# A mixture-of-experts decoder layer: residual rows kept in an array of sums, experts' outputs added to it by scatters

## What is computed

```python
x = _layernorm(x + attn(x, Wq, Wk, Wv, Wo, bo))
x = _layernorm(x + retention(x, ctx, ctx))
logits = x @ gate                       # 8 experts
weights, selected = top_k(logits, 2);  weights = softmax(weights)
g = x @ experts_w1[e];  u = x @ experts_w3[e]
eo[e] = (silu(g) * u) @ experts_w2[e]
x = _layernorm(x + sum over the two selected e of weight[e] * eo[e])
```

## Time and profile before

| | |
|---|---|
| median of 3 runs | 1004.99 us (1000.88 to 1008.09) |
| the profiled execution: time | 1007.5 us |
| its span in the profile | 1005.7 us |
| granted clock of PE over the span | 0.915 of full speed |
| PE busy | 804.7 us, 80% |
| DVE busy | 790.3 us, 79% |
| POOL busy | 652.6 us, 65% |
| ACT busy | 613.4 us, 61% |
| moved by DMA | 72.55 MB |

### The profile page before, as it was taken

One profiled execution on the slowest core, in us unless ns is written; L12 is line 12 of the kernel. 1 busy time (PEld: TensorE's weight loads), 2 busy tenths in 40 slices (PEclk: granted clock), 3 DMA queues, 4 the chain that ended last, 5 costly groups with the idle time before them and its releaser, 6 DMA issues.

```text
span 1005.7 us, 34508 instructions
## 1 busy us (share of the span) xinstructions
PE 804.7 (80%) x11940; PEld 603.2 (60%) x11940; DVE 790.3 (79%) x2155; ACT 613.4 (61%) x1416; POOL 652.6 (65%) x738
## 2 busy tenths in 40 slices
PE   1667799989999899898868660999999999999500
PEld 1345465656656556656544430799999999999500
DVE  4797799988999988998846644688888888888475
ACT  1133566768767777676666851676667666766355
POOL 0349767799999999998996456245444544454443
PEclk9788799999999999999987965899999999999855
DMA  9312222123232232221212004222222222222176
GB/s 307 81 29 54 40 48 50 42 62 70 51 71 62 54 74 52 61 58 42 63 39 62 23 22 91 58 61 66 63 62 61 66 63 61 62 65 58 53 252 226
DMA packets 145300, 72.55 MB, mean 72 GB/s; under 512 B 75024, under 2 KB 134544, under 8 KB 145136
## 3 DMA queue, kind: packets, MB, share of 16 engines
q1 hardware_dynamic: 124800, 40.43, 17.4%
q0 software_dynamic: 8640, 17.84, 5.4%
q10 hardware_dynamic: 11696, 12.08, 3.8%
HBM read 41.98 MB, written 28.34 MB: 70 GB/s over the span
## 4 chain that ended last, share of the span: by engine, by line
PE 38%; POOL 32%; issue 12%; DVE 3%; DMA 3%; ACT 2%; POOLq 0%; SPq 0%; ACTq 0%; DVEq 0%
POOL prod_ev L1536 17%; POOL routed_rows L1553 11%; PE QKV L773 9%; PE ST L773 9%; PE XT L801 6%; PE SC L801 5%; POOL rs L1516 3%; PE YY L589 2%; DMA prod_ev<-token_halves 2%; PE SC L560 1%; PE YY L791 1%; PE TR L791 1%; PE TR L606 1%; DMA routed_rows<-xe,pos 1%; PE TR L603 1%
## 5 line engine op out<-in xcount | busy, mean ns | idle before, releaser
L1536 POOL TENSOR_TENSOR prod_ev<-e_sb,q_v 128x512 f32<-128x512 f32 x256 | 300.2, 1206 | 70.5 <-PE YY L589 35.6
L1585 POOL DMA_INDIRECT token_halves<-w_new,tok_i x142 | 137.8, 971 | 32.5 <-issue 22.2
L1553 POOL DMA_INDIRECT routed_rows<-xe,pos x128 | 129.6, 1013 | 30.6 <-issue 29.9
L1151 DVE TENSOR_TENSOR prod_qk<-q_v,QKV 128x2048 f32<-128x2048 f32 x64 | 144.7, 2273 | 4.5 <-ACT q_v L870 4.5
L1438 DVE TENSOR_TENSOR prod_ev<-prod_qk,prod_ev 128x1024 f16<-128x1024 f32 x71 | 87.0, 1226 | 56.0 <-ACT prod_ev L1028 56.0
L1028 ACT CAST prod_ev<-prod_qk 128x1024 f16<-128x1024 f32 x71 | 74.2, 1045 | 76.0 <-DVE prod_qk L1464 51.4
L773 PE MATMUL QKV<-k_t,w_hl 128*128 128x256 f16 x852 | 116.8, 274 | 0.1
L773 PE MATMUL ST<-k_t,w_hl 128*128 128x256 f16 x852 | 116.7, 273 | 0.0
L409 POOL TENSOR_TENSOR marks<-half_c 128x1 f32<-128x1 f32 x103 | 19.9, 193 | 142.2 <-DVE w_new L1454 142.0
L1464 DVE SCALAR_TENSOR_TENSOR prod_qk<-ST,hid_scale,prod_qk 128x512 f32<-128x512 f32 x142 | 99.6, 744 | 2.3 <-ACT prod_qk L1037 2.3
L1037 ACT ACTIVATE prod_qk<-QKV,silu_scale 128x512 f32<-128x512 f32 x142 | 96.1, 678 | 8.6 <-PE QKV L773 4.6
(11 more groups left out here) (169 smaller groups left out, 1695.3 us busy)
## 6 DMA issues: line engine op xcount, KB each, us to landing
w_new<-routed_rows SPq DMA_DIRECT2D x71, 130.0 KB
prod_ev<-token_halves SPq DMA_DIRECT2D x16, 512.0 KB, 5.1
x_sb<-x SPq DMA_DIRECT2D x32, 128.0 KB, 3.0
x_res<-x SPq DMA_DIRECT2D x128, 32.0 KB
head_rows<-o_n SPq DMA_DIRECT2D x32, 128.0 KB
o_t<-head_rows SPq DMA_DIRECT2D x64, 64.0 KB
ctx_sb<-ctx SPq DMA_DIRECT2D x32, 128.0 KB, 2.7
out<-prod_qk ACTq DMA_DIRECT2D x16, 256.0 KB, 4.0
```

Of the source, the lines that this page charges most:

```text
L1151: eng.tensor_tensor(prod_qk[:, u, :, :].rearrange("p d (i j) -> p d i j", j=NH), q.unsqueeze(3).to_broadcast([P, HD, NH, NH]), k.unsqueeze ...
L1536: ins = eng.tensor_tensor(prod_ev[:, u, q, :, :, 0:HD], e_sb[:, it.slot(2), u, 64 * q:64 * q + 64].rearrange("p (i j) -> p j i", j=4).unsq ...
L1553: eng.indirect_dma_start(out=xs, out_offset=bass.IndirectOffsetOnAxis(ap=pos[:, r, 2 * u + k:2 * u + k + 1], axis=0), in_=xe[:, r, u, k, : ...
L1585: eng.indirect_dma_start(out=halves, out_offset=bass.IndirectOffsetOnAxis(ap=tok_i[:, s, u:u + 1], axis=0), in_=yw[:, s, u, :], in_offset= ...
```

## The change

The two half rows of a token in DRAM are gone. In their place stands `token_sums` with one row for each token. In stage A, SP writes the second norm's rows there once, four transfers a duo, 15 steps behind its first load. In stage B the experts' outputs, without `xh`, are added to these rows by POOL's scatters: the DMA reads the row, adds and writes it back. Since the two experts of a token can be in neighbouring tiles, each tile's scatters wait until those of the tile before have landed. In stage C one row a token is loaded (256 KB a chunk, ring of 8), DVE's addition is gone, and all 16 chunks are written out.

```diff
-        "spare_ids": 2 * n_tok + p[:, None] + P * np.arange(4 * n_exp)[None, :],
-        "ids": 2 * (P * b + row)[:, None] + 4 * P * (ids // 4) + 2 * S * (ids // 2 % 2) + ids % 2,
+        "spare_ids": n_tok + p[:, None] + P * np.arange(4 * n_exp)[None, :],
+        "ids": (P * b + row)[:, None] + 2 * P * (ids // 4) + S * (ids // 2 % 2),
...
-    PE_LAGS, ACT_LAGS, DVE_LAGS, POOL_LAGS, SP_LAGS = 13, 13, 14, 11, 9
-    CTX_LAG, HEADS_LAG = 9, 8
+    PE_LAGS, ACT_LAGS, DVE_LAGS, POOL_LAGS, SP_LAGS = 13, 13, 14, 11, 15
+    CTX_LAG, HEADS_LAG, ROWS_LAG = 9, 8, 15
...
-    C_FIRST, C_LAGS = 8, 3
+    C_RING = 8
+    C_FIRST, C_LAGS = n_chunks_c, 3
...
-    halves = nc.dram_tensor("token_halves", [2 * n_tok + 2 * n_exp * TILE, P], F32).ap()
+    token_sums = nc.dram_tensor("token_sums", [n_tok + 2 * n_exp * TILE, P], F32).ap()
...
+                if it := at(ROWS_LAG):
+
+                    r = it.slot(RING)
+                    wait(it, x2_ready)
+                    wait_dma(it, x2_out, 1, 64)
+                    for u in range(2):
+                        for b in range(2):
+                            eng.dma_start(x2_rows[it.number()][u][b], xe[S * u:S * u + S, r, b, 0, 0:P]).then_inc(x2_out, 16)
...
+            eng.wait_ge(x2_out, 64 * n_duo)
...
-                    wait(c, fout_ready, RING)
-                    eng.dma_start(fin[:, c.slot(RING), :, :, :],
-                                  half_rows[:, bass.ds(c.number() * C_SLICES, C_SLICES), :, :]).then_inc(fin_in[c.slot(RING)], 16)
+                    wait(c, fout_ready, C_RING)
+                    eng.dma_start(fin[:, c.slot(C_RING), :, :],
+                                  sum_rows[:, bass.ds(c.number() * C_SLICES, C_SLICES), :]).then_inc(fin_in[c.slot(C_RING)], 16)
...
                 wait_ring(it, routed_out, RING, 64)
+                wait_dma(it, x2_out, RING, 64)
...
-                    wait_ring(t, xg_in)
-                    wait(t, yw_ready, RING)
-                    eng.mul(xh[:, t.slot(RING), :, :], xg[:, t.slot(RING), :, 0:P], 0.5).then_inc(xh_ready, 1)
...
-                        ins = eng.scalar_tensor_tensor(out=yw[:, s, u, :], in0=YB[t.slot(2)][:, P * u:P * u + P],
-                                                       scalar=wt[:, s, u:u + 1], in1=xh[:, s, u, :], op0=ALU.mult, op1=ALU.add)
+                        ins = eng.tensor_scalar(yw[:, s, u, :], YB[t.slot(2)][:, P * u:P * u + P], wt[:, s, u:u + 1], None, ALU.mult)
...
-                    eng.tensor_tensor(y[:, :, 0, :], y[:, :, 0, :], y[:, :, 1, :], ALU.add).then_inc(fsum_ready, 1)
-                    wait(c, fsum_ready)
...
+                    wait_ring(t, half_out, 1, 32)
                     for u in range(2):
-                        eng.indirect_dma_start(out=halves, out_offset=bass.IndirectOffsetOnAxis(ap=tok_i[:, s, u:u + 1], axis=0),
-                                               in_=yw[:, s, u, :], in_offset=None).then_inc(half_out[s], 16)
+                        eng.indirect_dma_start(out=token_sums, out_offset=bass.IndirectOffsetOnAxis(ap=tok_i[:, s, u:u + 1], axis=0),
+                                               in_=yw[:, s, u, :], in_offset=None, compute_op=ALU.add).then_inc(half_out[s], 16)
```

More of the change, by code:

```diff
@@ L216, in build @@
     x_rows = x.rearrange("(n u b h g) d -> n u b g h d", u=2, b=2, h=NH, g=4)
-    half_rows = halves[0:2 * n_tok, :].rearrange("(p n k) d -> p n k d", p=P, k=2)
+    sum_rows = token_sums[0:n_tok, :].rearrange("(p n) d -> p n d", p=P)
+    x2_rows = token_sums[0:n_tok, :].rearrange("(n u b h g) d -> n u b g h d", u=2, b=2, h=NH, g=4)
     out_rows = out.rearrange("(p n) d -> p n d", p=P)
@@ L312, in in_new @@
             return w_new[:, at * RING * 2:(at + c) * RING * 2].rearrange("p (r u c) -> p r u c", r=RING, u=2)
-        xg, yw, xh = in_new(0, ROW), in_new(ROW, P), in_new(ROW + P, P)
+        xg, yw = in_new(0, ROW), in_new(ROW, P)
         x_hl = k_t[:, 0:2, :, :].rearrange("p r u t -> p (r u t)").bitcast(F16).rearrange("p (s k t) -> p s k t", s=2, k=2)
@@ L323, in build @@
         tok_i = sb("tok_i", [RING, 2], I32)
-        fin = stage_b2[:, 0:RING * C_SLICES * 2 * P].rearrange("p (r n k d) -> p r n k d", r=RING, n=C_SLICES, k=2)
+        fin = stage_b2[:, 0:C_RING * C_SLICES * P].rearrange("p (r n d) -> p r n d", r=C_RING, n=C_SLICES)
         fout = stage_b[:, 0:RING * C_SLICES * P].rearrange("p (r n d) -> p r n d", r=RING, n=C_SLICES)
@@ L380, in build @@
         x_in, ctx_in, routed_out = (ring_sem(n) for n in ("x_in", "ctx_in", "routed_out"))
+        x2_out = sem("x2_out")
         y_in = ring_sem("y_in")
@@ L389, in build @@
             [sem(f"{n}{half}") for half in range(2)] for n in ("g_done", "u_done", "sil_ready", "hid_ready"))
-        xhi_ready, xlo_ready, xh_ready, hhi_ready, hlo_ready = (
-            sem(n) for n in ("xhi_ready", "xlo_ready", "xh_ready", "hhi_ready", "hlo_ready"))
+        xhi_ready, xlo_ready, hhi_ready, hlo_ready = (
+            sem(n) for n in ("xhi_ready", "xlo_ready", "hhi_ready", "hlo_ready"))
         yw_ready, tok_ready, wt_ready = (sem(n) for n in ("yw_ready", "tok_ready", "wt_ready"))
-        fin_in, fin_out = ring_sem("fin_in"), ring_sem("fin_out")
+        fin_in, fin_out = [sem(f"fin_in{i}") for i in range(C_RING)], ring_sem("fin_out")
         fnb_ready = sem("fnb_ready")
-        fsum_ready, fstat_ready, fmv_ready, fve_ready, frs_ready, fout_ready = (
-            sem(n) for n in ("fsum_ready", "fstat_ready", "fmv_ready", "fve_ready", "frs_ready", "fout_ready"))
+        fstat_ready, fmv_ready, fve_ready, frs_ready, fout_ready = (
+            sem(n) for n in ("fstat_ready", "fmv_ready", "fve_ready", "frs_ready", "fout_ready"))
         marks = sb("marks", [7])
@@ L503, in load_tile @@
                     wait(t, xgt_done, RING)
-                    wait(t, xh_ready, RING)
                     wait(t, wt_ready, RING)
@@ L1047, in last_norm @@
                     for n in range(C_SLICES):
-                        ins = eng.activation(fout[:, r, n, :], fin[:, r, n, 0, :], ACT.Identity,
+                        ins = eng.activation(fout[:, r, n, :], fin[:, c.slot(C_RING), n, :], ACT.Identity,
                                              bias=fnb[:, s, n:n + 1], scale=frs[:, s, n:n + 1])
@@ L1449, in tile_step @@
                     wait(t, down_done)
-                    wait(t, xh_ready)
                     wait(t, wt_ready)
@@ L1471, in last_norm @@
                     s = c.slot(2)
-                    y = fin[:, c.slot(RING), :, :, :]
-                    wait_ring(c, fin_in)
-                    eng.tensor_tensor(y[:, :, 0, :], y[:, :, 0, :], y[:, :, 1, :], ALU.add).then_inc(fsum_ready, 1)
-                    wait(c, fsum_ready)
+                    eng.wait_ge(fin_in[c.slot(C_RING)], 16 * (c.off // C_RING + 1))
                     wait(c, fmv_ready, 2)
                     for n in range(C_SLICES):
-                        ins = eng.bn_stats(fstat[:, s, n, :], fin[:, c.slot(RING), n, 0, :])
+                        ins = eng.bn_stats(fstat[:, s, n, :], fin[:, c.slot(C_RING), n, :])
                     ins.then_inc(fstat_ready, 1)
```

## The result

The changed kernel takes 1077.96 us (median of 4 runs, 1074.38 to 1090.81) where the kernel before, on the same chip, takes 1006.54 (4 runs, 1000.88 to 1010.2). The ratio is 1.070, with a 95% interval from 1.063 to 1.077: slower by 7%. The forecast had the sign and the place, a loop through the new wait, but 1078 us lies 13 us above the top of its range (1065). The profiled execution of the changed kernel took 1074.38 us, 66.9 more than that of before (1007.5).

A forecast was written before the change was run, and what follows sets the result against it. PE bounds the experts' stage and transfers the last norm. From 1007.5 us profiled, minus 12.7 for the last norm, plus 31 for the scatter loop: 1025.8, as a median 1023 us. Range 990 to 1065.

The forecast's parts named there:

- The formula: Whole kernel: profiled time 945.6 + 71x us where the experts' scatter loop binds, x being the adding's cost per loop.
- Stage C: Last norm: 2.0 us a chunk and a first load landing after 3.5 us gain 12.7 us.
- The price x: Experts' stage: what adding costs per scatter loop, longer issue on both scatters plus longer landing; taken as 1.13 us.
- half of the load trip: Experts' scatters: fetching the old row adds half of a 2.25 us load trip, 1.13 us, to each loop.
- doubled descriptors: Upper case for the experts' scatters: POOL writes twice the descriptors, adding another 2 x 0.98 us per loop.
- the rival: Experts' stage: the wait is hidden, x below 0.73; 996.3 us profiled, 994 as a median; chance 0.35.
- The room of 0.7 us: Experts' stage: the plain scatter loop with the wait takes 3.65 us, about 0.7 under PE's 4.37 us a tile.
- x = 0.73 and 0.87: Adding cost per loop in us: below 0.73 the kernel is faster by over 1%, at 0.87 it breaks even.
- "hidden": Experts' stage: scatters land before PE's next output, x below 0.73; median 994 us; chance 0.35.
- cost 0: Stage A: SP's four new stores a duo need 2.3 us of about 10 free, so they cost nothing.
- the bound of 14: Stage A: at most 14 us if new stores delay the routing scatter 28 times by 0.5 us each.
- The rival that named them: Stage A: new stores make routed rows land 0.5 us later in 28 duos, 14 us; median 1008; chance 0.04.

The follow-up runs named there:

- e7: The changed kernel with the second adding scatter of each tile cut to 64 of its 128 rows: 1057.24 us (one run).
- e1: The changed kernel with odd tiles' adds going to a second, unread array and each tile waiting two tiles back: 999.25 us against 1004.87, ratio 0.993.
- e2: The changed kernel with plain scatters that overwrite instead of adding, the wait for the tile before kept: 1002.53 us, ratio 0.994.
- e3: The kernel before with only the wait for the tile just before added, scatters plain: 1013.24 us against 1007.20, ratio 1.0053.
- e9: The kernel before with SP's 128 new stores, into an unread array, plus their step lag and waits: 1012.97 us against 1007.20, ratio 1.0046.
- e11: The changed kernel waiting for the tile just before only at an expert's first tile, token-number ring of eight, first four tiles free: 1013.05 us against 1005.81.

## Why the prediction was right or wrong

**What bounded the kernel, and where the change would act: right.** The stage bound by PE turned into one bound by the loop of wait and scatter; the last norm got shorter; PE's busy share fell under 0.9.

**The formula: right.** It says 945.6 + 71x. With the measured x = 5.47 - 3.65 = 1.82 it gives 1074.8; the profiled execution took 1074.4. That it fits to 0.4 us is partly luck: the last tile starts 1.1 us later than 644.0 + 70 x 5.47, and what follows is 1.5 us shorter than forecast. Stage C came within 1.5 us of the forecast (14.2 against 12.7): a chunk in 1.91 us, as the loop through bn_aggr said, and the first load lands after 2.69 us, not 3.5. Its DMA share, which I expected to stay high, fell to 0.66: with half the bytes it is paced by that loop.

```profile
1049.28 0.20 POOL L1599 TENSOR_TENSOR fve<-fmv,eps_c 128x4 f32<-128x4 f32 x1 [0.63 <-DVE fmv L1494]
...
1051.19 0.20 POOL L1599 TENSOR_TENSOR fve<-fmv,eps_c 128x4 f32<-128x4 f32 x1 [0.63 <-DVE fmv L1494]
```

**The price x: the step that failed.** I took 1.13, "half of the load trip", and left longer issues to the upper bound, tied there to doubled descriptors. The rows after give 1.82, made otherwise:

| part of the loop | forecast | measured | source |
|---|---|---|---|
| wake after the landing | 0.12 | 0.27 | chain: 0.03 + 0.02 + 0.04 + 0.18 |
| first scatter to second | 1.28 | 1.87 | 1028.04 to 1029.91 |
| second issue to landing, of it the issue | 0.96 | 1.56 | timeline |
| ... and the rest | 1.29 + 1.13 | 1.77 | 3.33 - 1.56 |
| sum | 4.78 | 5.47 | |

The way after the issue, on which I had put the whole price as a trip to the old row in memory, is longer by 0.48 us (1.77 - 1.29), less than half of what I took; whether that is a trip or the larger number of packets is open, though e7, with 0.31 less at half the rows, speaks for a price by rows in part. Both issues together cost 1.19 more, on which I had put nothing. The other 0.15 are the wake, and not the adding. At 71 turns the difference, 0.69 us, is 49 us, nearly all of the miss (1074.4 - 1025.8 = 48.6).

The Trainium skill, Collectives: The Full Stack (The bandwidth ceiling), which stood for the rival, prices the stream: the add itself is free, the second source read halves the rate. By that, x would have been near 0.24, an estimate; measured, it is 1.82. e1 shows only that the stage has room for the longer transfers (PE full, no time lost), and the issue on POOL is no part of the stream.

**The room of 0.7 us: too large, and not safe.** In e2 the plain loop is 3.78 us where DVE leaves POOL alone, so the room is 0.6. e2 and e3 use it for 16 and 22 tiles; after one late landing the scatters start during DVE's subtraction, the loop takes PE's 4.37, and the room is gone. So the thresholds at x = 0.73 and 0.87 were too kind, and "hidden" at 0.35 was too likely.

**Stage A: cost 0 was wrong by a little.** The stores find SP free as read, but lengthen the wait before the second norm; e9 puts them at 2 to 7.5 us, under the bound of 14. The rival that named them had the right place, at up to about half of its price; that the routing scatters land later, as it said, is not shown.

**The range.** It ended at x = 1.72. My own upper rows reached far above (2.25, and 2 x 0.98 more), and I gave the part above 1.72 a chance of 0.12. The bound for issues should have been taken as a live case: an operation that no row shows has an issue as well as a transfer, and POOL's issue stood twice in the loop.

## What to carry to other kernels

When a change puts a wait for a transfer's landing into a loop, add up the whole loop: wake, every issue of the engine in it, and landing, each at the price it has for the new kind of transfer and beside the neighbours it will then have. Here a bare wait with plain scatters left 0.6 us of PE's tile, lost after the first late landing, and 0.6 us more on each of two issues, with 0.5 on the landing, repeated 71 times, cost more than five times what the last stage gained. Adding scatters here needed tiles that can overlap: with two arrays they cost no time in that stage.

## What the runs showed that I had not expected

An adding scatter of 128 rows takes POOL 1.57 us to issue, a plain one 0.98, also when DVE is idle (1028.04 above), and 64 rows instead of 128 save only 0.13. It is cut into more packets: leaving out the 128 routing scatters at 32 packets each, (24,544 - 128 x 32) / 142 = 144 an adding scatter, where a plain one has 32 (8,640 / 270).

A scatter that is issued while DVE's subtraction of two arrays in SBUF is already running gets longer by nearly the rest of it: 0.60 us with 0.73 left at 818.42 (e2), 0.27 with 0.40 left at 771.38 (e3), 0.55 with 0.68 left at 796.24 (e11, adding). Overlap alone doesn't do it: in e1 the subtraction starts at 805.27, 0.13 us after the second scatter, runs wholly inside it, and the scatter takes its 1.56, as do the second scatters of nearly all tiles there. So in these rows what counts is which of the two starts first, and what is held up lies near the start of the issue; which part of it that is stays open. The Trainium skill, GPSIMD Engine Reference (Specifications), counts DVE instructions with two SBUF inputs among those that contend with POOL; e2, e3 and e11 agree, and e1 shows an overlap without a loss. The Trainium skill, DMA: Bandwidth & Descriptors (SWDGE vs HWDGE vs iDMA), says that POOL writes its descriptors into SBUF state that DVE locks it out of in its 2-port mode; e1, where the subtraction covers most of an issue that takes no longer, speaks against that as the cause here. No run took the subtraction away, so that it is the cause is argued from the overlaps and not shown by itself.
